# A graph, attention and mixture-of-experts block on one core: one head on each half of the PE array, and another order in the opening

## The reference, cut to what matters

```
xn = layernorm(x)                                    # x: 1250 nodes x 512, f32
# graph part: 40000 edges src -> dst
agg[n] = mean of xn[src] over the edges with dst = n
gnn = relu(layernorm(xn @ w_self.T + agg @ w_neigh.T + bias) * gamma + beta)
# linear attention, 8 heads of 64
q, k, v = split(xn @ w_qkv)
q_phi = elu(q @ proj_mat[h]) + 1;  k_phi = elu(k @ proj_mat[h]) + 1
kv[h] = k_phi[h].T @ v[h]                            # 64 x 64 over all nodes
z = 1 / (q_phi @ sum of k_phi over the nodes)
mix = (q_phi @ kv * z) @ w_proj + b_proj
x = x + gnn + mix
x = x + ffn(layernorm(x))                            # shared expert and 8 routed ones, top 2
```

## Time and profile before

| what | value |
|---|---|
| time, median of 3 runs | 781.32 us (780.72 to 784.39) |
| the profiled execution's own time | 779.41 us |
| its span, first to last instruction | 777.6 us |
| PE busy | 734.0 us (94%) |
| PE weight loads (PEld) | 456.4 us (59%) |
| DVE busy | 409.9 us (53%) |
| ACT busy | 262.7 us (34%) |
| POOL busy | 168.0 us (22%) |
| mean granted TensorE clock | 0.982 of full speed |

### The profile page before, as it was taken

One profiled execution on the slowest core, in us unless ns is written; L12 is line 12 of the kernel. 1 busy time (PEld: TensorE's weight loads), 2 busy tenths in 40 slices (PEclk: granted clock), 3 DMA queues, 4 the chain that ended last, 5 costly groups with the idle time before them and its releaser, 6 DMA issues.

```text
span 777.6 us, 11923 instructions
## 1 busy us (share of the span) xinstructions
PE 734.0 (94%) x4217; PEld 456.4 (59%) x4217; DVE 409.9 (53%) x809; ACT 262.7 (34%) x387; POOL 168.0 (22%) x167
## 2 busy tenths in 40 slices
PE   4998999998799999999999999999889999999998
PEld 4664777775457755656575654445745555555554
DVE  4877987795457766696435442222146434421154
ACT  2761222222255223236534213333345524422000
POOL 3320000000006000002222224444612222211462
PEclk9999999999999999999999999999969999999999
DMA  9200002000004114001234320111367866333674
GB/s 239 91 1 0 1 2 79 31 1 1 13 2 135 55 62 156 1 0 27 54 98 145 107 54 17 46 48 55 109 211 247 324 234 231 122 122 125 191 206 133
DMA packets 24368, 73.37 MB, mean 94 GB/s; under 512 B 7138, under 2 KB 7484, under 8 KB 20225
## 3 DMA queue, kind: packets, MB, share of 16 engines
q1 hardware_dynamic: 8607, 39.74, 15.3%
q0 software_dynamic: 10624, 24.99, 11.1%
q10 hardware_dynamic: 5090, 8.01, 2.8%
HBM read 57.38 MB, written 15.31 MB: 93 GB/s over the span
## 4 chain that ended last, share of the span: by engine, by line
PE 77%; DVE 9%; ACT 7%; DMA 3%; issue 2%; ACTq 1%; POOL 0%; DVEq 0%; POOLq 0%
PE banks L1272 58%; PE banks L1314 6%; PE banks L1302 6%; PE banks L1611 2%; DMA y_rows<-xT 1%; ACT W L411 1%; PE banks L1327 1%; DMA big<-in_proj_mat 1%; DVE st L733 1%; PE banks L1295 1%; DVE W L710 1%; PE banks L1482 1%; DVE xn L1092 1%; ACT big L579 1%; ACTq L457 1%
## 5 line engine op out<-in xcount | busy, mean ns | idle before, releaser
L1272 PE MATMUL banks<-W,xT 128*125 128x512 f16 (+1 forms) x1392 | 319.9, 384 | 8.0 <-ACT xT L677 1.9
L1272 PEld LDWEIGHTS banks<-W,xT 128*125 128x125 f16 (+1 forms) x1392 | 166.0, 122 | 139.0 <-issue 17.6
L1272 PE MATMUL banks<-xT,W 128*128 128x500 f16 (+1 forms) x720 | 131.3, 344 | 1.8 <-DVE xn L1224 1.4
L1272 PEld LDWEIGHTS banks<-xT,W 128*128 128x128 f16 x720 | 70.7, 98 | 60.4 <-issue 4.4
L710 DVE SCALAR_TENSOR_TENSOR W<-stg,W 128x2048 f16<-128x2048 f32 x30 | 68.8, 2313 | 42.7 <-ACT W L411 42.7
L1272 PE MATMUL banks<-W,big 128*125 128x512 f16 x360 | 81.5, 380 | 0.0
L1242 DVE CAST xT<-banks 128x1024 f32 x23 | 28.1, 1222 | 73.4 <-PE banks L1611 73.4
L1272 PEld LDWEIGHTS banks<-W,big 128*125 128x125 f16 x360 | 48.3, 136 | 29.2 <-issue 2.3
L353 POOL DMA_INDIRECT xn<-h_rows,tokidx x28 | 35.1, 1253 | 125.8 <-PE banks L1611 119.6
L342 POOL TENSOR_TENSOR big<-xn,big 125x512 f16<-125x512 f32 x20 | 23.5, 1173 | 173.1 <-ACT big L594 173.1
L411 ACT ACTIVATE W<-stg 128x2048 f16<-128x2048 f32 x30 | 56.4, 1904 | 0.0
(11 more groups left out here) (292 smaller groups left out, 861.3 us busy)
## 6 DMA issues: line engine op xcount, KB each, us to landing
stg<-in_units SPq DMA_DIRECT2D x30, 1024.0 KB, 5.0
y_rows<-xT ACTq DMA_DIRECT2D x29, 256.0 KB
h_rows<-big POOLq DMA_DIRECT2D x10, 500.0 KB, 3.6
out_x<-x SPq DMA_DIRECT2D x10, 224.0 KB
stg<-in_wqkT SPq DMA_DIRECT2D x2, 1024.0 KB, 11.5
x<-in_x SPq DMA_DIRECT2D x2, 896.0 KB
x<-in_x SPq DMA_DIRECT2D x1, 448.0 KB
xn<-h_rows,tokidx POOLq DMA_INDIRECT x28, 5.2
```

The costliest lines, as they stand in the source:

```text
L1272: ins = te.matmul(dst, lhs(sl, c), rhs(sr, c), start=(first and c == 0 and k == 0), stop=(last and c == n - 1 and k == 2))
```

## The change

Six edits, none of which alters what is computed:

1. `kvacc` and `att` treat each head by itself. In `kvacc` a head's 64 features are the weights and 65 columns (64 of v, one of ones) the moving operand; even heads use the left half of the array's columns and lanes 0 to 63 of the bank, odd ones the right half and lanes 64 to 127 (`tile_position`). In `att` a head's 64 features are the rows, so even heads use the upper and odd ones the lower half of the array, and the two halves write to different banks. A tile takes 8 products of 65 columns in place of 4 of 129 or 130. `kvbd` has no zeros any more: one copy in place of eight, and its clearing on POOL goes.
2. The four first folds stand in a row, behind the transposes of tiles 0 and 1 instead of before them; ACT and DVE follow that order. `proj_mat` comes by two DMAs in place of eight.
3. ACT does `rows_high` later and in another grouping; `key_relu(0)` and `key_relu(1)` stand ahead of the square root of the later tiles, and POOL starts its low parts only when all ten tiles are normalised.
4. PE takes the products with the masks after the count of g = 2 instead of g = 1, and `kvacc(3)` after the count of g = 0.
5. `spread` writes to bank 4 and bank 5 in turn, and waits for the copy of two blocks ago instead of one.
6. The run-time loop uses `CT[1]` and bank 5 (the last written-out block has `CT[0]` and bank 4), and PE reads its trip count before the last `spread` instead of after it.

```diff
@@ -433,12 +433,19 @@
                              bank.rearrange("p (c n) -> p c n", c=C), ACT.Copy, scale=WS).then_inc(S["wp_h"], 1)
 
             def key_phi(t):
+                key_relu(t)
+                key_exp(t)
+
+            def key_relu(t):
                 o = 1024 * (t % KTMP)
                 act.wait_ge(S["k_mm"], t + 1)
...
+                o = 1024 * (t % KTMP)
                 act.wait_ge(S["k_neg"], t + 1)
                 s.activation(ktmp[:, o:o + 512], ktmp[:, o:o + 512], ACT.Exp, scale=-1.0).then_inc(S["k_exp"], 1)
...
                              scale=1 / WS).then_inc(S["v_ev"], 1)
 
             act.wait_ge(S["pool_bd"], 1)
-            for h in range(HEADS):
-                r, o = h // 2, HD * (h % 2)
-                act.dma_start(projbd[o:o + HD, r, o:o + HD], a["proj_mat"][h]).then_inc(S["ld_bd"], 16)
+            pm = a["proj_mat"].rearrange("(r h) d f -> h d r f", h=2)
+            for h in range(2):
...
             act.wait_ge(S["pool_const"], 1)
             s.activation(ident16[:, :], ident[:, :], ACT.Copy).then_inc(S["id_rdy"], 1)
             sqrts(*GROUPS[0])
+            xT_high(0)
+            xT_high(1)
...
             xT_high(3)
-            for t in range(4):
-                rows_high(t)
+            rows_high(0)
+            key_relu(0)
+            rows_high(1)
+            rows_high(2)
+            key_relu(1)
             sqrts(*LATER)
-            key_phi(0)
-            key_phi(1)
+            key_exp(0)
+            key_exp(1)
             xT_high(4)
...
             key_phi(2)
-            rows_high(4)
-            rows_high(5)
             xT_high(6)
             xT_high(7)
             key_phi(3)
-            rows_high(6)
...
-            rows_high(7)
             unit(U_V)
+            rows_high(3)
+            rows_high(4)
             xT_high(8)
             xT_high(9)
             key_phi(4)
-            rows_high(8)
-            rows_high(9)
+            for t in range(5, TILES):
+                rows_high(t)
...
@@ -505,7 +514,7 @@
...
-                s.activation(aggacc[0:BLK, i, :], ps[4][0:BLK, :], ACT.Copy).then_inc(S["agg_ev"], 1)
+                s.activation(aggacc[0:BLK, i, :], ps[4 + i % 2][0:BLK, :], ACT.Copy).then_inc(S["agg_ev"], 1)
...
@@ -767,19 +776,17 @@
...
-            wp_low(0, ps[2])
-            dve.wait_ge(S["ld_x1"], 16 * len(PARTS))
-            v.bn_stats(st[:, 4, :], x[:, 4, :])
-            v.bn_stats(st[:, 5, :], x[:, 5, :])
-            wp_low(1, ps[7])
             xT_low(0)
             xT_low(1)
+            wp_low(0, ps[2])
+            wp_low(1, ps[7])
             wp_low(2, ps[3])
-            v.bn_stats(st[:, 6, :], x[:, 6, :])
-            v.bn_stats(st[:, 7, :], x[:, 7, :])
             wp_low(3, ps[6])
             xT_low(2)
             xT_low(3)
+            dve.wait_ge(S["ld_x1"], 16 * len(PARTS))
+            for t in range(4, 8):
+                v.bn_stats(st[:, t, :], x[:, t, :])
...
@@ -979,29 +986,22 @@
...
-                        for z in range(2):
-                            kv2 = kvb[z][:, 0:258].rearrange("p (r n) -> p r n", r=2)
-                            for h in range(2):
-                                q = slice(HD * h, HD * h + HD)
-                                v.tensor_copy(kvbd[q, 2 * z:2 * z + 2, HD * h:HD * h + HD], kv2[q, :, HD * h:HD * h + HD]).then_inc(S["kvbd_rdy"], 1)
-                                v.tensor_copy(kvbd[q, 2 * z:2 * z + 2, 128 + h:129 + h], kv2[q, :, 128:129]).then_inc(S["kvbd_rdy"], 1)
+                        v.tensor_copy(kvbd[:, :, :], kvb[0][:, 0:PAIRS * (HD + 1)].rearrange("p (r n) -> p r n", r=PAIRS)).then_inc(S["kvbd_rdy"], 1)
 
...
-                for z in range(2):
-                    pa = ps[2 * (t % 2) + z][0:P, 0:260].rearrange("p (r n) -> p r n", r=2)
-                    zz = rs[:, 6 + t % 2, 4 * z:4 * z + 4].rearrange("p (r h) -> p r h", r=2)
-                    if z == 0:
...
+                    if t >= 2 and h == 0:
                         dve.wait_ge(S["tT_mm"], t - 1)
-                    pa = ps[2 * (t % 2) + z][0:P, 0:260].rearrange("p (r n) -> p r n", r=2)
-                    zz = rs[:, 6 + t % 2, 4 * z:4 * z + 4].rearrange("p (r h) -> p r h", r=2)
-                    v.tensor_tensor(attn(t)[:, z].rearrange("p (r h n) -> p r h n", r=2, h=2),
-                                    pa[:, :, 0:128].rearrange("p r (h n) -> p r h n", h=2),
-                                    zz.unsqueeze(3).to_broadcast([P, 2, 2, HD]), ALU.mult).then_inc(S["at_rdy"], 1)
+                    pa = ps[2 * (t % 2) + h][0:P, 0:PAIRS * (HD + 1)].rearrange("p (r n) -> p r n", r=PAIRS)
+                    zz = rs[:, 6 + t % 2, 4 * h:4 * h + 4]
+                    v.tensor_tensor(attn(t).rearrange("p z (r h n) -> p (z r) h n", r=2, h=2)[:, :, h], pa[:, :, 0:HD],
+                                    zz.unsqueeze(2).to_broadcast([P, PAIRS, HD]), ALU.mult).then_inc(S["at_rdy"], 1)
 
...
@@ -1323,9 +1323,11 @@
...
                 for r in range(PAIRS):
-
-                    ins = te.matmul(kvb[r // 2][:, (r % 2) * 129:(r % 2) * 129 + 129], kph[t % KPH][:, r * 128:(r + 1) * 128],
-                                    scr_v(t)[:, r, :], start=(t == 0 and r % 2 == 0), stop=(t == TILES - 1), skip_group_check=True)
+                    for h in range(2):
+                        q = slice(HD * h, HD * h + HD)
+                        n = 2 * r + h
+                        ins = te.matmul(kvb[0][q, r * (HD + 1):(r + 1) * (HD + 1)], kph[t % KPH][:, n * HD:(n + 1) * HD], scr_v(t)[:, n, :],
+                                        start=(t == 0 and r == 0), stop=(t == TILES - 1), skip_group_check=True, tile_position=(0, HD * h))
                 ins.then_inc(S["kvacc_mm"], 1)
 
...
@@ -1349,15 +1351,15 @@
             pe.wait_ge(S["pool_const"], 2)
             for k in range(WARM):
                 te.matmul(ps[5][:, 0:128], ident[:, :], tri[:, :], start=True, stop=True)
+            turn_x(0)
+            turn_x(1)
             pe.wait_ge(S["ld_wk"], 16)
-            pe.wait_ge(S["ld_bd"], 16 * HEADS)
+            pe.wait_ge(S["ld_bd"], 16 * 2)
             fold(0, ps[2])
             fold(1, ps[7])
-            turn_x(0)
-            turn_x(1)
             fold(2, ps[3])
+            fold(3, ps[6])
             turn_x(2)
-            fold(3, ps[6])
             turn_x(3)
             keys_mm(0)
...
@@ -1413,8 +1414,8 @@
...
-                        if i >= 2:
-                            pe.wait_ge(S["agg_ev"], i - 1)
+                        if i >= 3:
+                            pe.wait_ge(S["agg_ev"], i - 2)
...
@@ -1422,6 +1423,8 @@
                     keys_mm(KEY_AT[g])
                 if g in VAL_AT:
                     values_mm(VAL_AT[g])
+                if g == 0:
+                    kvacc(3)
...
@@ -1430,22 +1433,21 @@
                         pe.wait_ge(S["k_rel"], TILES)
                     pe.wait_ge(S["wp_rdy"], FOLD_AT[g])
                     fold(FOLD_AT[g], ps[6])
+            items = pe.value_load(tab[0:1, 2 * ITEMS:2 * ITEMS + 1], min_val=1, max_val=ITEMS)
             pe.wait_ge(S["ct_rdy"], 3 * FIX)
+            pe.wait_ge(S["agg_ev"], FIX - 2)
+            spread((FIX - 1) % 2, deg=FIX - 1).then_inc(S["agg_mm"], 1)
+
             pe.wait_ge(S["agg_ev"], FIX - 1)
-            spread((FIX - 1) % 2, deg=FIX - 1).then_inc(S["agg_mm"], 1)
-
-            pe.wait_ge(S["tab_rdy"], 1)
-            pe.wait_ge(S["agg_ev"], FIX)
-            items = pe.value_load(tab[0:1, 2 * ITEMS:2 * ITEMS + 1], min_val=1, max_val=ITEMS)
             with pe.Fori(0, items) as i:
                 for j in range(SUBS):
                     pe.wait_ge(S["x_oh"], i * SUBS + (j + 1))
...
                 pe.wait_ge(S["x_ct"], i * 3 + 3)
                 pe.wait_ge(S["x_add"], i * 2 + 2)
-                spread(0)
+                spread(1)
                 for t in range(TILES):
-                    ins = te.matmul(kvb[0][0:BLK, 420:421], CT[0][0:P, t, :], ones16[0:P, 0:1], start=(t == 0), stop=(t == TILES - 1))
+                    ins = te.matmul(kvb[0][0:BLK, 420:421], CT[1][0:P, t, :], ones16[0:P, 0:1], start=(t == 0), stop=(t == TILES - 1))
...
@@ -1479,8 +1481,10 @@
...
                 for r in range(PAIRS):
-                    ins = te.matmul(ps[2 * (t % 2) + r // 2][0:P, (r % 2) * 130:(r % 2) * 130 + 130],
-                                    qphi[:, r, t * P:(t + 1) * P], kvbd[:, r, :], start=True, stop=True)
+                    for h in range(2):
+                        q = slice(HD * h, HD * h + HD)
+                        ins = te.matmul(ps[2 * (t % 2) + h][0:P, r * (HD + 1):(r + 1) * (HD + 1)], qphi[q, r, t * P:(t + 1) * P], kvbd[q, r, :],
+                                        start=True, stop=True, tile_position=(HD * h, 0))
```

More of the change, by code:

```diff
@@ L143, in build @@
         projbd = big[:, 7 * 1024:8 * 1024].bitcast(F32).rearrange("p (r n) -> p r n", r=PAIRS)
-        kvbd = sb("kvbd", [128, PAIRS, 130])
+        kvbd = sb("kvbd", [128, PAIRS, HD + 1])
```

(12 more changed lines are left out.)

35 lines of the change are left out of this document (19 added, 16 removed).

## The result

The changed kernel takes 773.46 us, median of 4 runs (771.67 to 776.86), where the kernel before, run beside it, takes 782.86 (780.72 to 784.67): a ratio of 0.9886, 95% interval 0.9838 to 0.9934, or 9.4 us less. The forecast was 772.0. The execution that was profiled is the longest of the four, 776.86, with a span of 774.9; its rows follow. A second set of six runs of the same kernel, with another profile, comes as the first experiment, and what the two traces differ in turns out to be half of the story.

A forecast was written before the change was run, and what follows sets the result against it. PE bounds the kernel, busy 734.0 of 777.6 us. Terms 6.3 + 1.35 + 0.4 + 2.3 - 1.1 = 9.3 off 779.4 give 770.1; with the median 1.9 above, 772 (own range 769 to 775, overall 765 to 780.5).

The forecast's parts named there:

- a start of g = 4 after 79: Graph stage: the count of g = 4 was forecast at 76.3 us; starting after 79 would make the forecast wrong.
- Opening: Start of the kernel: folds from 14.8 to 19.4 us, first keys at 20.6 instead of 23.49, 2.9 us sooner.
- gain here: 1.8 us: Opening: a new 2.2 us wait on PE, with keys of tile 6 starting at 44.4 instead of 46.2.
- Halves: `kvacc` and `att`: array halves run side by side, so `kvacc` takes 0.62 us and `att` 1.03 a tile.
- rival 1: `att`: row halves load one after the other, column halves run together; gain only 1.8 us, 779.5; chance 0.17.
- rival 3: `kvacc` and `att`: every head's change of position drains the array; slower, 785 to 796 us; chance 0.09.
- 1.1 us lost: Attention: `att` on halves takes 0.14 us more on each of the eight tiles behind the first two.
- 0.27 less, ten times 2.7 us: `kvacc` on halves takes 0.62 us, 0.27 less a tile, over ten tiles 2.7 us.
- Masks: Graph stage: masks start at 63.9 us instead of 68.44, and PE waits 1.8 before the count of g = 2.
- I take the clock to stay up, since the new wait is shorter by 1.0: Graph stage: no lower granted clock behind the new 1.8 us wait, 1.9 of the 7.0 us gained at g = 4.
- rival 2: Opening and graph: ACT's `rows_high` push more than PE, or PE's clock falls behind a new wait; 776 us; chance 0.15.
- 2.3 plus 0.4 forecast: Before the run-time loop: 2.3 us from waits at the last `spread` and loop start, 0.4 from two banks.

The follow-up runs named there:

- experiment 1: The changed kernel run again without any edit, with a second profile: 774.75 us, ratio 0.9903 to the kernel before.
- experiment 8: The changed kernel with ACT doing the Relus of tile 5 ahead of the five `rows_high`: 774.86 us, ratio 0.9924 to the kernel before.
- experiment 2: The kernel before with only the halves (`kvacc`, `att` and `kvbd` as after): 783.18 us, ratio 0.9996 to the kernel before.
- experiment 5: The changed kernel with all even heads first, then all odd ones, in `kvacc` and `att`: 779.93 us, one run.
- experiment 6: The kernel before with halves, two banks for `spread`, the loop's other buffers and early register load, without opening and later masks: 778.28 us, ratio 0.9960.
- experiment 7: The changed kernel with two buffers for an expert's result, ACT copying before it waits for the previous store: 772.17 us, ratio 0.9887 to the kernel before.
- experiment 3: The changed kernel with `att` back on the whole array and `kvacc` on halves: 768.62 us, ratio 0.9822 to the kernel before.

## Why the prediction was right

The forecast was 772.0, a gain of 9.3; it came out at 773.46, and at 774.75 in the second set (gains of 9.4 and 7.5 over the runs beside them). The mechanisms were nearly all as described, but that the sum fits the medians this well is in part luck. Up to the mark the profiled executions gain 9.2 and 5.1 us; behind it they give back 4.3 and 2.4, which wasn't in the forecast. So their spans are only 4.9 and 2.7 us shorter, half of the 9.3 or less. In the medians that is made up for on the other side: the kernel before's profiled execution, 779.41, was a fast one (its medians are 780.85 to 782.86) without a slow store, and its other executions have no trace. The prediction's own sign of being wrong, a start of g = 4 after 79, came in the first trace (79.52) and not in the second (76.10).

- **Opening.** First keys at 18.77, not 20.6: the folds start at 13.69, so `projbd` is there by then and not at 14.8, and the four of them take 3.59 us, not 4.6. The wait before `keys_mm(6)` was 2.01 us (2.2), its start 42.52 (44.4). The step "gain here: 1.8 us" failed in what it stands for: measured there the gain is 3.7, yet the count of g = 0 starts at 62.53 (62.9), because DVE's edge chain and not this wait sets the pace up to there (experiment 8). Even the half clock behind it in the first trace cost only 0.24 us at the count of g = 0 (62.53 against 62.29 in experiment 1).
- **Halves.** `kvacc` 0.62 and `att` 1.02 were forecast as 0.62 and 1.03. Rivals 1 and 3 fall (experiments 2 and 5): row halves overlap as column halves do, and a head in turns costs less than a head in a row. The mechanism was right; two terms were mis-sized. The Trainium skill, in "TensorEngine Tiling (Array Packing)", Key Properties, says that tiles load and multiply in parallel, and the trace agrees: 0.064 us per product in turns, 0.094 on one half. One is "1.1 us lost": a tile takes 0.28 more, not 0.14, so eight take 2.2. The forecast's 1.03 was to hold both changes between whole and half (0.83 and 0.2); by starts `att` takes 1.02 without them, and they come on top, some 0.1 ahead of `att` and 0.05 in `att_turn`, together what the bias product gave, 0.14. The other is "0.27 less, ten times 2.7 us": the 0.10 ahead of `kvacc` was left out, so a tile saves 0.17 (experiment 2). The halves were to bring 1.6 us and bring nothing.
- **Masks.** Starts of the masks 63.76 (63.9), wait before the count of g = 2 1.86 (1.8). "I take the clock to stay up, since the new wait is shorter by 1.0" is the step that failed: in the first trace it fell (0.76 from 70 to 84 us), and the count of g = 4 came at 79.5 instead of 76.3; in the second, behind the same 1.86 us, it stayed, and the count came at 76.10. So the clock of rival 2 came true in one execution and not in the other, of one kernel.
- **Loop.** 2.3 plus 0.4 forecast; 3.3 in the traces, 2.8 by the ratios, which know it to some 3 us (experiment 6). The loop starts 8.0 us sooner in the first trace and 10.9 in the second, forecast 10.35.
- **Queries.** The forecast left them out. The means' wait of 3.16 us is as long as before, and behind it and the next wait products of 2.5 us took 4.96 and 4.02 in the first trace, 4.17 and 2.54 in the second. The kernel before pays that too (4.23 and 4.00), so it moves the difference by less than 2.
- **Experts.** Not in the forecast either: 2.4 and 4.3 us given back mostly where ACT waits for a store that takes 7.1 instead of 5.7 us (experiment 7).

By parts, in ratios: the halves 0 (experiment 2), banks and loop 2.8 (experiment 6). Opening and masks are what the changed kernel has more than experiment 6, 4.5 or 5.8 us by its two ratios, each known to some 4; in the traces the count of g = 4 starts 3.0 and 6.4 us sooner than there (79.52 and 76.10 against 82.50). The two were never run apart.

What stays open: why the clock falls behind one wait and not behind the same wait in another execution, and why a store takes 7.1 us in some places; both differ between executions of one kernel. Nor is it known whether the kernel before has as many slow stores in its other executions, since only one was traced; the opening and the masks don't make them (experiment 7).

## What to carry to other kernels

Take two profiles before you put down to a change what lies far behind it: two executions of one kernel differed by 4 us at one mark. A wait of PE is priced by who would be next: one of 2 us was worth nothing, while products of no use placed in the waits, which make none of these waits end sooner, brought 3.1 us at the mark against one execution and 7.2 against the other. Give heads a half of the array each where the products' columns set the pace and the load is short (`kvacc`, 0.17 us less a tile), but count the change of mode on both sides; keep the whole array where the load of weights does (`att`), and let heads take turns between the halves.

## What was not expected of the hardware

- Going from the whole array to halves cost 0.10 us ahead of `kvacc` (0.56 from start to start instead of 0.46, experiment 2) and some 0.1 ahead of `att` (2.70 instead of 2.60); on the way back the four transposes took 0.48 instead of 0.42 (first trace and experiment 3).
- After waits of the same length, 1.86 us, the granted clock was 0.76 in one execution (70 to 84 us) and 1.00 in another.
- In one execution (experiment 1) the same store of 256 KB took 5.6 to 6.0 us at some places and 7.1 at others; behind the long ones PE was idle for 1.6 us, behind the others for 0.2 to 0.5.
